# Moving steps of a slot-scheduled kernel: key transposes, first rows, self attention and last statistics

## The reference

```
x = x + xattn(layernorm(x), ctx, mask)   # rmsnorm of both sides, 4 query heads of 128, one key/value head,
                                         # rope, masked softmax over 1601 context rows, output product
x = x + attn(layernorm(x))               # causal self attention, 16 heads of 32, within each sequence
x = x + ffn(layernorm(x))                # W_fc (2048x512), exact gelu, layernorm over 2048, W_proj (512x2048)
```

## Time and profile before

| what | us |
|---|---|
| median of 3 runs | 1073.27 (1072.84 to 1074.04) |
| the profiled execution | 1072.88 |
| its span in the trace | 1071.0 |
| TensorE busy | 930.1 (87%) |
| VectorE busy | 668.2 (62%) |
| ScalarE busy | 504.6 (47%) |
| GpSimd busy | 376.0 (35%) |

### The profile page before, as it was taken

The page is one execution under the profiler, slowest core; times in us unless marked ns, Lnnn a source line. Parts: engine busy times, 40 slices in busy tenths (PEclk is TensorE's granted clock), DMA queues, the critical chain, the costliest instruction groups (busy, mean ns, idle before and its releaser), DMA issues. The chain is left out here.

```text
span 1071.0 us, 22550 instructions
## 1 busy us (share of the span) xinstructions
PE 930.1 (87%) x7307; PEld 699.8 (65%) x7307; DVE 668.2 (62%) x1334; ACT 504.6 (47%) x1059; POOL 376.0 (35%) x506
## 2 busy tenths in 40 slices
PE   3798879898788888868959999999889999999996
PEld 3787667686576776657948887988765444444443
DVE  5577766766676767675275656666656448475543
ACT  4565445654455544544332323343446455556542
POOL 2354444444444444440021111111203325444434
PEclk9899999999999999979969999999989999999998
DMA  6521223221222322331444444444422102112011
GB/s 178 182 75 56 79 88 89 87 68 43 80 86 76 94 62 76 114 114 41 97 142 129 133 125 139 114 124 112 121 68 70 60 1 82 38 40 69 21 60 43
DMA packets 100318, 93.02 MB, mean 87 GB/s; under 512 B 45424, under 2 KB 61904, under 8 KB 100176
## 3 DMA queue, kind: packets, MB, share of 16 engines
q1 hardware_dynamic: 99376, 90.96, 28.8%
q10 hardware_dynamic: 672, 0.26, 0.1%
q0 software_dynamic: 128, 0.03, 0.0%
HBM read 74.37 MB, written 12.66 MB: 81 GB/s over the span
## 5 line engine op out<-in xcount | busy, mean ns | idle before, releaser
L255 PE MATMUL bank<-f,f 128*128 128x256 f32 (+4 forms) x5032 | 635.6, 302 | 70.1 <-issue 26.0
L255 PEld LDWEIGHTS bank<-f,f 128*128 128x128 f32 (+3 forms) x5032 | 459.4, 161 | 197.2 <-issue 81.4
L244 DVE TENSOR_TENSOR f<-bank,f 128x512 fp32r<-128x512 f32 x211 | 140.4, 683 | 49.3 <-ACT f L241 47.3
L241 ACT ACTIVATE f<-bank 128x512 fp32r<-128x512 f32 x211 | 121.1, 591 | 94.8 <-PE bank L230 89.6
L230 PE MATMUL bank<-f,f 128*128 128x128 f32 x896 | 133.7, 281 | 34.1 <-DVE f L244 13.5
L230 PEld LDWEIGHTS bank<-f,f 128*128 128x128 f32 x896 | 103.5, 143 | 57.1 <-issue 31.9
L1248 PE MATMUL bank<-f,f 128*128 128x512 f16 x512 | 123.0, 384 | 0.0
L1221 POOL TENSOR_TENSOR f<-f,f 128x512 f32<-128x512 f32 x59 | 75.1, 1272 | 133.1 <-ACT f L1216 133.1
L1226 DVE SCALAR_TENSOR_TENSOR f<-bank,f,f 128x512 f16<-128x512 f32 x64 | 47.9, 749 | 92.2 <-ACT f L1208 75.8
L954 POOL TENSOR_TENSOR f<-f,f 128x512 f32<-128x512 f32 x32 | 33.4, 1043 | 186.2 <-DVE f L951 186.2
L463 POOL TENSOR_TENSOR f<-f,f 128x512 f32<-128x512 f32 x32 | 42.0, 1311 | 158.9 <-ACTq L75 136.5
(11 more groups left out here) (138 smaller groups left out, 995.2 us busy)
## 6 DMA issues: line engine op xcount, KB each, us to landing
f<-in_ctx_dram SPq DMA_DIRECT2D x71, 256.0 KB, 2.8
f<-x_scratch SPq DMA_DIRECT2D x64, 256.0 KB, 3.6
x_scratch<-f SPq DMA_DIRECT2D x32, 256.0 KB, 2.0
f<-in_L_ffn_W_fc_dram SPq DMA_DIRECT2D x32, 256.0 KB, 2.8
f<-in_L_ffn_W_proj_dram SPq DMA_DIRECT2D x32, 256.0 KB, 3.4
f<-in_x_dram SPq DMA_DIRECT2D x31, 256.0 KB, 3.0
f<-in_ktab_dram SPq DMA_DIRECT2D x71, 64.0 KB, 2.0
f<-f SPq DMA_DIRECT2D x64, 64.0 KB, 2.5
```

What stands on the lines that cost most here:

```text
L241: return maybe("act", lambda e: e.activation(hi, src, ACT.Copy), sem(name + "_hi"), waits, when)
L244: return maybe("dve", lambda e: e.tensor_tensor(lo, src, hi.bitcast(F32), ALU.subtract), sem(name + "_lo"), waits, when)
L255: f = lambda e, i=i, a=a, b=b: e.matmul(dst, a, b, start=(first and i == 0), stop=(last and i == n - 1), skip_group_check=check)
```

## The change

Six edits of bookings, no arithmetic changed. (1) `stage_KT` goes from slot s0+6 to s0+7 and its `lo` from s0+7 to s0+8, for all batches but the last; the two other writers of the bank are booked behind it, `stage_Q1b` at s0-4, order 1 (was s0-5, order 8) and `stage_Q3` at s0, order 2 (was s0-1, order 8). (2) The x rows of pair 1 are loaded ahead of the second context instead of behind the third, and the first two masks behind the second context. (3) The first key/value products come ahead of the first query projection, and the rests of the query weights are made in two slots of the main list. (4) B2 falls by 7 slots, and `s2_late` with it. (5) `s3_scale` goes from B2+4 to B2+30. (6) `s3_stat` goes ahead of all output products that are left, takes the squares' sums first (which wait for less), and the products go tile by tile.

```diff
@@ stage_KT
-        at(b * FT + 7, 0.5, low)
+        at(b * FT + (8 if b + 1 < nb else 7), 0.5, low)
@@ masks
+    def first_masks():
+        for b in range(2):
+            done["msk", b] = load_mask(b)
     def stage_mask(b):
-        t = load_mask(b)
+        t = done["msk", b] if b < 2 else load_mask(b)
@@ weights of the queries
-    tw1["q"] = scaled_lo(wq_t, WQh, WQl, [t_wq, t_r1], t_qh)
+    def stage_WQ(c):
+        tw1["q"] = scaled_lo(wq_t, WQh, WQl, [t_wq, t_r1], t_qh, [c])
     for c in range(4):
+        at(-1 + c // 2, 4, lambda c=c: stage_WQ(c))
+    at(-11, 2.65, first_masks)
@@ the bookings of cross attention
-        at(s0 + 4 if b > 0 else -1, 1.7, lambda b=b: stage_mask(b))
+        at(s0 + 4, 1.7, lambda b=b: stage_mask(b))
-        at(s0 + 6, 4, lambda b=b: stage_KT(b))
+        at(s0 + (7 if b + 1 < nb else 6), 4, lambda b=b: stage_KT(b))
-                at(s0 - 12, 1.4, lambda i=i: load_xq(i))
+                at(s0 - 12 if i > 1 else -11, 1.4 if i > 1 else 1.65, lambda i=i: load_xq(i))
-                at(s0 - 5, 8, lambda i=i: stage_Q1b(i))
-            at(s0 - 3, 8, lambda i=i: stage_Q2(i))
-            at(s0 - 1, 8, lambda i=i: stage_Q3(i))
+                at(s0 - 4, 1, lambda i=i: stage_Q1b(i))
+            at(s0 - 3 if i else 1, 8, lambda i=i: stage_Q2(i))
+            at(s0 if i else 3, 2, lambda i=i: stage_Q3(i))
@@ self attention and the scale
-    T0, B2 = FT * nb + 2, FT * nb + 24
+    T0, B2 = FT * nb + 2, FT * nb + 17
-    at(T0 + 20, 8.9, s2_late)
+    at(T0 + 13, 8.9, s2_late)
-    at(B2 + 4, 4.6, s3_scale)
+    at(B2 + 30, 4.6, s3_scale)
@@ the end
     def s3_plast():
-        for t in (2, 3):
-            s3_p(last - 1, [t])
         for t in range(4):
-            s3_p(last, [t])
+            for q in (last - 1, last):
+                s3_p(q, [t])
     def s3_stat(g):
-        w = [*tok["acc", g], *tok["acc2", g], *gfree[k], t_on]
-        for t in range(4):
-            for z in range(2):
+        w = {1: [*tok["acc2", g], *gfree[k], t_on], 0: tok["acc", g]}
+        for z in (1, 0):
+            for t in range(4):
...
-    at(H0 + last + 2, 2.1, lambda: s3_p(last - 1, [0, 1]))
```

More of the change, by code:

```diff
@@ L669, in scaled_hi, with scaled_lo @@
                    sem("hi"), waits) for c in range(4)]
-    def scaled_lo(src, hi, lo, waits, ths):
-        for c in range(4):
+    def scaled_lo(src, hi, lo, waits, ths, chunks=range(4)):
+        for c in chunks:
             tl = op("dve", lambda e, c=c: e.scalar_tensor_tensor(
@@ L1281, in s3_stat @@
                         bank[k][:, z * 4 + t:z * 4 + t + 1], a, ones[:, 0:1], start=n == 0, stop=n == m,
-                        skip_group_check=True), sem("f_p") if t == 3 and z and n == len(parts) - 1 else None,
-                        w if t + z == 0 else ())
+                        skip_group_check=True), sem("f_p") if t == 3 and not z else None,
+                        w[z] if t + n == 0 else ())
         tok["stat", g] = [tk]
```

## The result

The changed kernel takes 1235.74 us (1235.05 to 1236.60) against 1073.40: 1.1515 times the time of before, 95% interval 1.1498 to 1.1531. The forecast was 1192.4 us, with a range up to 1235. The direction and the loop were right; the size was too small by 43 us, just outside the range.

What follows compares the result with a forecast made beforehand. TensorE was taken to set the pace in cross attention, though not full. 1072.9 + 92.4 (waits) + 47.6 (clock) - 5 (first batches) - 15 (seam) - 0.5 (end) = 1192.4 us; range 1150 to 1235, or 1110 to 1235 with (a).

Steps and rivals of the forecast that it cites:

- the loop: Cross attention rounds: second logits, exponentials, L518, rope, keys' rest part, Q1b or Q3, key/value products, again second logits; 6.85 us to Q1b/Q3.
- (b): Rival, cross attention rounds: no loop, the keys' rest part comes early enough; 1046 us, chance 0.17.
- (d): Rival: the edit does nothing, misc[0] holding an older token; within 0.2% of before, chance 0.02 shared with loop and gains balancing.
- (a): Rival, cross attention rounds: the stalls come but TensorE's clock holds; 1145 us, chance 0.25.
- (c): Rival, cross attention: the clock never comes back in the 28 rounds; 204 us lost instead of 48, about 1349 us, chance 0.01.
- The wait's term: Cross attention: TensorE stands still about 4.1 us a round, net 3.3 after savings; 28 rounds, 92 us.
- Two steps come in: Chain from second logits to Q1b/Q3: keys' hi part before second exponential (0.60), rest part behind L467 (0.68), making 6.85 us.
- at some 2.7: Cross attention rounds: TensorE by itself would arrive at Q1b or Q3 some 2.7 us behind the second logits.
- The number of rounds: Cross attention: the loop runs from the first logits to the last query, slots 12, 16, up to 120, 28 times.
- The clock's term: Cross attention: TensorE runs at low clock behind each stall, losing 1.7 us a round; 48 us, between 0 and 81.
- The first batches: Start of the kernel: sooner load of pair 1's rows removes L601's wait and its low clock; -5 us, between -2 and -8.
- The seam: Between the two attentions: TensorE's idle time and low clock mostly go with self attention seven slots sooner; -15 us, -8 to -19.

Runs made afterwards that it cites:

- the filled wait: The changed kernel with 20 additional unused 128x512 matmuls on TensorE in the wait of each of batches 0 to 25: 1188.8 us, ratio 1.108.

## Where the prediction was right, and which of its terms failed

**The loop: right.** Every link stood in the trace as forecast: the hi part ahead of the second exponential, the rest part behind L467, TensorE waiting at Q1b and Q3, each round, and in the 26 rounds for no other computing engine. Undoing the one edit gives 1063.2 us, making it alone 1245.8. The rivals without the loop (b) and (d) are out; so is (a), since the clock does fall (0.82), and (c), since it comes back in each round (twelve products take 2.91 us and the next twelve 1.70). In one of the 29 rounds the clock doesn't fall at all: behind a wait of 2.94 us the transposes at 291.03 take 0.63.

**The wait's term: too small, 3.3 us a round against 4.2 (4.3 by the windows).** This is the term that failed. TensorE stands still for 5.3 us a round, not 4.1; its waits in the 26 rounds:

```profile
PE bank L230 <- DVE f L244: 138.3, 26, 6.2
```

Two steps of the prediction are in it. The first is "Two steps come in". A third thing came in: L467 itself, costed at 0.83 us from the rows of before, takes 1.48 in 26 of the 29 rounds. VectorE and GpSimd weren't apart before. L465 met the end of GpSimd's L463, and L467 met L476, which had 0.56 us left. The hi part holds the second exponential and L518 back, so the rope comes one GpSimd operation later: L465 meets L476 (408.50), and L467 meets L478 and waits out its 1.20 us. From the logits to Q1b it is 7.45 us in the round shown and 7.35 in the mean of 28, not 6.85. The 6.0 us chain of the earlier trace rows was no sign of this, its L467 takes 0.83 us too; the sign stood at 41.06 and 52.66 us of the kernel before, where L467 takes 1.52 us beside L463. L476 of the batch in the earlier trace rows, and the second of these two L467:

```profile
365.60 0.79 POOL L476 TENSOR_SCALAR f<-f 128x512 fp32r<-128x512 f32 x1
```

```profile
52.66 1.52 DVE L467 TENSOR_TENSOR f<-f,f 128x256 f32<-128x256 f32 x1
```

The second step is TensorE's own arrival, "at some 2.7" us behind the logits. It is there at 2.1 in the mean (7.35 less 5.3), and at 1.57 in the round shown. What the prediction took off the wait for work and waits moved out of the rest of the round, some 0.8 us, comes to 1.0 (5.3 less 4.3).

**The number of rounds: 29, not 28.** I let the loop begin with the first exponential, at slot 12. TensorE already waits 4.47 us at slot 8, at Q3 behind the first keys' rest part, which there queues on VectorE behind the rope and a rest of the output weights:

```profile
51.83 0.68 DVE L244 TENSOR_TENSOR f<-bank,f 128x512 fp32r<-128x512 f32 x1
52.66 1.08 PE L230 MATMUL bank<-f,f 128*128 128x128 f32 x4 [4.47 <-DVE f L244]
```

This first one isn't the keys' alone: with the keys back and the other edits in, TensorE waits 3.77 us at about the same place (50.10).

**The clock's term: right.** 1.7 us a round from one row of before; measured 1.8 by the filled wait and 1.7 by the windows. The half of the throttled time by the Trainium skill's section (TensorE: Matmul & The Clock Gate, "HAM oscillation — how this bites in real kernels") gave 2.05, a little more; the measurements are nearer to the row.

**The first batches: -5 forecast, -3.3 by the trace, -1.1 alone** (interval -2.9 to 0). The removed wait is gone; what was late next was not followed far enough. Besides the context tiles, which I named, the split of the output weights stands in front of the first key transposes on ScalarE, and their load is issued behind the fourth context:

```profile
44.96 0.63 ACT L241 ACTIVATE f<-f 128x512 fp32r<-128x512 f32 x1 [4.75 <-DMA f<-in_L_xattn_out_w_dram]
```

**The seam: -15 forecast, -5.6 alone** and -7.0 less 1.9 in the changed kernel. This is the worst term. I summed the idle time and the low clock of a stretch (18 us) and left 3 of it. But by their releasers the waits of 1 to 2 us belong to chains of the first tiles (exponential, layernorm, rest part), and the clock falls behind them here as in the rounds: 0.82, where the forecast had it at 1. What went is the wait of s3_scale (4.09) and part of the first softmax's (3.69 to 2.1). That nothing more was there to be won is argued, not shown. The +1.9 at the last logits is the same mechanism as in the rounds, a wait of 7.41 us for the late rest part of batch 30 instead of two waits of 2.3; the forecast stopped at the last query and missed it.

**The end: -0.5 forecast, -0.7 by the trace**, too small for the time to show.

In one sum: 29 x 5.94 = 172.3 instead of 140.0 for the rounds (+32.3), +1.7 for the first batches, +9.9 for the seam with the last logits, -0.2 for the end: 43.7 us more than the forecast's 119.5, which makes the 163.2 of the spans. The range's upper end fell short because I combined its bounds as if they were independent. The rounds' two bounds (3.8 and 2.9 us) and the smallest gain of the seam (8 us) would have given some 1247; the rounds' two share one cause, the length of the loop and what follows from TensorE standing still, and so they come together. Of what the profile was to show, the rounds were to be 17 to 19 us and are 20.2; the clock of 7 to 9 tenths, the waits of L518, and the missing waits of s3_scale and L601 came as forecast.

## What to carry to other kernels

When a step is booked later in a list that runs in order, look at what now stands in front of it on every engine it uses, and then at who waits for it: if that is an instruction of the engine that sets the pace, walk the loop from there back to itself and add it up; its length is the new round. Durations in that sum are those of the new neighbourhood, not of the old one: an operation may meet another neighbour now, and wait for it. And a stretch with idle time isn't worth its idle time: take it only for the waits whose releaser the change removes.

## What the runs showed of the hardware

VectorE's 128x256 float32 product of two operands (L467) took 0.42 us alone. When one of GpSimd's 128x512 operations was under way as it started, it ended some 0.3 us behind that operation's end, in all but one of 352 such cases: 0.83 us with 0.56 left, 1.48 with 1.20 left. It took 28.4 us out of one kernel to move GpSimd's two steps away. And 520 matmuls that nobody uses made a kernel faster by 46.9 us: the mean granted clock went from 0.90 to 0.97, with 1.00 over a wait behind which it had been 0.50. The clock isn't fixed by the wait alone. Behind equal waits (1.09 and 1.06 us) the same twelve products took 3.05 and 4.58 us in two kernels, and behind a wait of 2.94 us in the changed kernel it didn't fall, behind one of 3.05 it did.
